# Attention B of a two-layer block: q, k and v at their own width of 64, heads worked in pairs

## The reference

```
x = x + attn_a(layernorm(x))
x = x + ffn(layernorm(x))
x = x + attn_b(layernorm(x))
x = x + ffn(layernorm(x))

attn_b(r):   # 16 heads of width 64
    q, k, v = r @ Wq + bq, r @ Wk + bk, r @ Wv + bv      # per head: 256 x 64
    pattern = softmax(causal(q @ k.T / 8))               # 256 x 256
    out = sum over heads of (pattern @ v) @ Wo  + bo     # 256 x 128
```

## Time and profile before

| | |
|---|---|
| time, median of 3 runs | 453.93 us (453.14 to 454.97) |
| the profiled execution's span | 451.1 us |
| beside its span | the time of that one execution is not listed by itself; the three timed runs lie 2.0 to 3.9 us above the span |
| PE busy | 405.4 us, 90% |
| PE weight loads busy | 359.2 us, 80% |
| ACT, DVE, POOL busy | 310.5, 307.7, 34.1 us |
| first scores, last weighted sum | 63.6 us, 424.4 us |

### The profile page before, as it was taken

How to read it: one execution, slowest core, us unless ns; L and a number is a source line. 1 busy time by engine, 2 the same in 40 slices (tenths; PEclk the granted TensorE clock), 3 DMA queues, 4 the chain that set the end, 5 groups by cost and what they waited for, 6 DMA issues and landing times.

```text
span 451.1 us, 8672 instructions
## 1 busy us (share of the span) xinstructions
PE 405.4 (90%) x2591; PEld 359.2 (80%) x2591; DVE 307.7 (68%) x1322; ACT 310.5 (69%) x945; POOL 34.1 (8%) x48
## 2 busy tenths in 40 slices
PE   0857688999999999999999999999999999999766
PEld 0756677878889988888899889888899898999545
DVE  4465538666878776977777858886786687766542
ACT  1443158797868897976768887876688888778420
POOL 4030100100000000200000002000000000000000
PEclk9998869999999999999999999999999999999955
DMA  8600000000000000000000000000000000000000
...
DMA packets 8157, 5.68 MB, mean 13 GB/s; under 512 B 944, under 2 KB 7856, under 8 KB 8112
## 3 DMA queue, kind: packets, MB, share of 16 engines
...
## 4 chain that ended last, share of the span: by engine, by line
PE 75%; ACT 10%; DVE 7%; issue 4%; DMA 2%; POOL 0%; ACTq 0%; DVEq 0%
PE bank L452 11%; PE bank L283 9%; PE bank L284 9%; PE bank L285 9%; PE bank L437 9%; PE bank L361 6%; PE bank L454 5%; PE bank L427 5%; PE bank L390 2%; DVE gated L698 2%; ACT prob L571 2%; PE bank L351 2%; DMA wv<-wv_in 2%; PE bank L306 2%; ACT gate_t L537 1%
## 5 line engine op out<-in xcount | busy, mean ns | idle before, releaser
L579 ACT ACTIVATE prob_t<-bank 128x384 f32<-128x384 f32 x128 | 62.8, 490 | 22.7 <-PE bank L437 22.5
L452 PE MATMUL bank<-prob_t,v 128*128 128x256 f32 x256 | 76.5, 381 | 0.7 <-ACT o_t L604 0.7
L437 PE MATMUL bank<-ident,prob 128*128 128x128 f32 x384 | 63.8, 275 | 4.7 <-ACT prob_t L579 4.6
L571 ACT ACTIVATE prob<-neg_s,neg_max 128x256 f32<-128x256 f32 x128 | 64.3, 503 | 0.0
L569 ACT ACTIVATE prob<-neg_s,neg_max 128x128 f32<-128x128 f32 x128 | 51.5, 403 | 12.3 <-DVE neg_max L737 12.0
L735 DVE CUSTOM_DVE_ANT_0 neg_s<-bank,mask 128x128 f32<-128x128 f32 x128 | 36.7, 287 | 33.8 <-PE bank L285 33.8
L437 PEld LDWEIGHTS bank<-ident,prob 128*128 128x128 f32 x384 | 45.4, 140 | 15.1 <-DVE prob L746 5.0
L454 PEld LDWEIGHTS bank<-prob_t,v 128*128 128x128 f32 x256 | 48.5, 190 | 6.7
L737 DVE CUSTOM_DVE_ANT_0 neg_s<-bank,mask 128x256 f32<-128x256 f32 x128 | 53.7, 420 | 0.0
L427 PE MATMUL bank<-rt,u 128*128 128x128 f32 x256 | 49.8, 276 | 0.8 <-DVE neg_max L737 0.8
L454 PE MATMUL bank<-prob_t,v 128*128 128x128 f32 x256 | 49.1, 274 | 0.0
...
## 6 DMA issues: line engine op xcount, KB each, us to landing
...
```

Of the source, the lines that this page charges most:

```text
L437: last = nc.tensor.transpose(pt_ps[:, j * P:(j + 1) * P], prob[:, k % 4, j * P:(j + 1) * P], ident[:])
L452: nc.tensor.matmul(o_ps[:, b * N:(b + 1) * N], vg[:, 2 * b, hs], prob_t[:, k % 2, 0:N], start=(step == 0), stop=False, skip_group_check=True)
L571: nc.scalar.activation(prob[:, q, P:SC], neg_s[:, r, P:SC], ACT.Exp, bias=neg_max[:, q, 1:2], scale=-1.0, accum_out=row_sum[:, q, 1:2]).th ...
L579: nc.scalar.activation(prob_t[:, k % 2, :], pt_ps[:, 0:SC], ACT.Copy).then_inc(pt_sb, 1)
```

## The change

- q, k and v are computed with the plain weights, 64 wide for a head, two heads side by side on the 128 partitions ("unit": 8 in a pair). Jobs qp and kp (X and Y) each make q^T or k^T of a unit for 512 tokens; vpX and vpY make v of 8 heads for one tile. The jobs w0 to w5 only split the weights in two halves (ACT and DVE); the products that built M and WVO are gone, and so are wb, u_low and the second copy of lntB.
- A slot is one unit and one batch: 16 slots in a pair, 64 in all, each with two heads e = 0, 1. The scores of head e contract over the 64 partitions of half e (HALVES), all in float32: rows 0 to 63 and rows 64 to 127 of PE. The weighted sum of head e has 64 output columns, which go to partitions 0 to 63 or 64 to 127 of z_ps.
- z of each unit is copied to zt by ACT (z_evac, a ring of 10), and multiplied by Wo per unit with accumulation: jobs out0 to out3, one a tile, 8 products of a tile each, and outA to outD for the last pair.
- qp, kp, vpX, vpY and the out jobs share the banks X and Y with the side jobs. Three banks now hold scores, two the transposed probabilities.
- The probabilities are scaled by POOL. Of the transposed probabilities ACT copies head 0, DVE head 1. DVE reads out kp, ACT qp, v and z.
- The transposes and the sums run LAG = 2 slots behind the scores. In a slot each engine walks its head, then the jobs of that slot (projections first, then BODY), then its tail.
- In the prologue the ACT queue issues three transfers of 512 KB (wqkv) in place of wo and two halves of wv; the SP queue issues wo, bq, bk, bv, bo in place of wk, two halves each of wq and bq, bv and bo, and no longer waits for POOL's zero fills. In EPILOGUE outB and outD stand for the two bout jobs. bo is added by POOL in lntB. The store to memory is issued in the same job as before.

```diff
 PAIRS = B * N // PAIR
 TILES = PAIR // P
 FC = F // P
-STEPS = 2 * H
-GH = PAIR // D
-GROUPS = H // GH
-CH = GROUPS * TILES
+UNITS = H // 2
+SLOTS = 2 * UNITS
+LAST = PAIRS * SLOTS
+LAG = 2
+GV = PAIR // A
+CHUNKS = H // GV * TILES
+ZR = 10
 SC = N + P
+HALVES = (slice(0, A), slice(A, P))
 EPS = 1e-5
 W_SCALE = 1.0 / 127.0
 SCORE_SCALE = A ** -0.5
...
 BODY = {
-    1: [("lns0", 1)], 3: [("lns1", 1)], 4: [("lntA", 1)], 5: [("qkv0", 1), ("qkv1", 1)], 6: [("qkv2", 1)], 7: [("mean", 1)],
-    8: [("bout", -1)], 9: [("lns0", -1)], 10: [("vwo", 1), ("lns1", -1)], 11: [("lntF", -1), ("mat0", 1)], 12: [("mat1", 1)],
-    13: [("gu0", -1)], 15: [("aout", 1), ("gu1", -1)], 17: [("lns0", 1), ("gu2", -1)], 18: [("lns1", 1)],
-    19: [("down", -1), ("lntF", 1)], 20: [("gu0", 1)], 21: [("gu1", 1)], 22: [("gu2", 1)], 23: [("down", 1)],
-    24: [("lns0", 1)], 25: [("lns1", 1)], 26: [("lntB", 1)],
+    0: [("lns0", 1), ("lns1", 1)], 1: [("lntA", 1)], 2: [("qkv0", 1), ("qkv1", 1), ("out0", -1)],
+    3: [("qkv2", 1), ("mean", 1), ("out1", -1)], 4: [("vwo", 1), ("mat0", 1), ("out2", -1)],
+    5: [("mat1", 1), ("out3", -1), ("lns0", -1)], 6: [("aout", 1), ("lns1", -1), ("lntF", -1)],
+    7: [("lns0", 1), ("gu0", -1)], 8: [("gu1", -1), ("lns1", 1)], 9: [("gu2", -1), ("lntF", 1)],
+    10: [("down", -1), ("gu0", 1)], 11: [("gu1", 1), ("gu2", 1)], 12: [("down", 1), ("lns0", 1)],
+    13: [("lns1", 1), ("lntB", 1)],
 }
-U_AHEAD, V_AHEAD = 3, 4
-T_LAG, PV_LAG = 3, 4
...
+def projections_at(m):
+
+    jobs = []
+    if 0 <= (m + 2) // 8 < 2 * PAIRS and (m + 2) % 8 < TILES:
+        jobs.append(("vpY" if m % 2 == 0 else "vpX", TILES * ((m + 2) // 8) + (m + 2) % 8, 0))
+    g, odd = divmod(m + 2, 2)
+    if g < PAIRS * UNITS:
+        jobs.append(("kp" if odd else "qp", g, 0))
+    return jobs
+
+
+def jobs_at(m):
+
+    jobs = projections_at(m)
+    p, i = divmod(m, SLOTS)
+    if m >= 0 and p < PAIRS:
+        for job, off in BODY.get(i, []):
+            if 0 <= p + off < PAIRS:
+                t0 = (p + off) * TILES
+                jobs.append((job, t0 + int(job[3]), 1) if job.startswith("out") else (job, t0, TILES))
+    if m == LAST - 1:
+        jobs += [("outA", LAST_TILE, 2), ("outC", LAST_TILE + 2, 2)]
+    return jobs
+
+
+LAST_TILE = (PAIRS - 1) * TILES
 
...
-        s_ps, pt_ps, u_ps, v_ps, o_ps, X, Y = bank[0:2], bank[2], bank[3], bank[4], bank[5], bank[6], bank[7]
...
+        s_ps, pt_ps, z_ps, X, Y = bank[0:3], bank[3:5], bank[5], bank[6], bank[7]
...
+        def s_bank(m, e):
+
+            return s_ps[(2 * m + e) % 3]
+
...
+            for m in range(-2, LAST + LAG):
+                head(m, at)
+                for job, t0, nt in jobs_at(m):
+                    side(job, t0, nt, at)
+                    at.passed(job, t0, nt)
+                tail(m, at)
...
+                elif job in ("out0", "out1", "out2", "out3", "outA", "outB", "outC", "outD"):
+                    p = t0 // TILES
+                    first = OUT_EARLY if job in ("outB", "outD") else 0
+                    end = OUT_EARLY if job in ("outA", "outC") else UNITS
+                    out, done = (Y, y_full) if job in ("outC", "outD") else (X, x_full)
+                    pe.wait_ge(z_sb, p * UNITS + end)
+                    if job == "outC":
+                        use_y(at)
+                    elif first == 0:
+                        use_x(at)
+                    for u in range(first, end):
+                        for j in tiles:
+                            last = nc.tensor.matmul(out[:, j * D:(j + 1) * D], zt[:, (p * UNITS + u) % ZR, j * P:(j + 1) * P], wo[:, u, :],
+                                                    start=(u == 0 and j == tiles[0]), stop=(u == UNITS - 1), skip_group_check=True)
+                    if end == UNITS:
...
+                elif job in ("qp", "kp"):
+                    p, u = divmod(t0, UNITS)
+                    if t0 == 0:
+                        pe.wait_ge(w_lo, 4 if job == "kp" else 2)
+                    if u == 0:
+                        rows_ready(p, at)
+                    if job == "qp":
+                        use_x(at)
+                        out, done, w = X, x_full, 0
+                    else:
+                        use_y(at)
+                        out, done, w = Y, y_full, 1
+                    us = slice(u * P, (u + 1) * P)
+                    split3(out[:], wqkv_hi[:, w, us], wqkv_lo[:, w, us], rt_hi[:, p % 2, :], rt_lo[:, p % 2, :]).then_inc(done, 1)
...
+                elif job in ("vpX", "vpY"):
+                    p, c = divmod(t0, CHUNKS)
+                    g, j = divmod(c, TILES)
+                    if t0 == 0:
+                        pe.wait_ge(w_lo, 6)
+                    if c == 0:
+                        rows_ready(p, at)
+                    if job == "vpX":
+                        use_x(at)
+                        out, done = X, x_full
+                    else:
+                        use_y(at)
+                        out, done = Y, y_full
+                    hs = slice(g * GV * A, (g + 1) * GV * A)
+                    js = slice(j * P, (j + 1) * P)
+                    split3(out[:], rt_hi[:, p % 2, js], rt_lo[:, p % 2, js], wqkv_hi[:, 2, hs], wqkv_lo[:, 2, hs]).then_inc(done, 1)
 
             def rows_ready(p, at):
...
+            def scores(m, at):
+
+                g, b = divmod(m, 2)
+                if b == 0:
+                    pe.wait_ge(x_free, at.mark["qp", g].x)
+                    pe.wait_ge(y_free, at.mark["kp", g].y)
+                if m:
+                    pe.wait_ge(s_masked, 2 * m - 1)
...
+                for e, half in enumerate(HALVES):
+                    nc.tensor.matmul(s_bank(m, e)[:, 0:P], qt[half, g % 2, t:t + P], kt[half, g % 2, t:t + P], start=True, stop=True)
+                for e, half in enumerate(HALVES):
+                    nc.tensor.matmul(s_bank(m, e)[:, P:SC], qt[half, g % 2, t + P:t + N], kt[half, g % 2, t:t + N],
+                                     start=True, stop=True).then_inc(s_full, 1)
...
+            def transposes(m):
+
+                for e in range(2):
+                    pe.wait_ge(p_norm, 2 * m + e + 1)
+                    if m:
+                        pe.wait_ge((pt_sb_a, pt_sb_b)[e], m)
+                    for j in range(3):
+                        last = nc.tensor.transpose(pt_ps[e][:, j * P:(j + 1) * P], prob[:, m % 3, e, j * P:(j + 1) * P], ident[:])
+                    last.then_inc(pt_full, 1)
...
+            def weighted_sum(m, at):
+
+                g, b = divmod(m, 2)
+                group = m // 8
+                pe.wait_ge(pt_sb_a, m + 1)
+                pe.wait_ge(pt_sb_b, m + 1)
+                if m % 8 < 2:
+                    pe.wait_ge(x_free, at.mark["vp", TILES * group + 2 * b + 1].x)
+                    pe.wait_ge(y_free, at.mark["vp", TILES * group + 2 * b + 1].y)
+                if b == 0 and g:
+                    pe.wait_ge(z_sb, g)
+                for k, cols in ((0, slice(0, N)), (1, slice(N, SC))):
+                    for e, half in enumerate(HALVES):
+                        h = (2 * g + e) % GV
+                        last = nc.tensor.matmul(z_ps[half, b * N + k * P:(b + 1) * N], v[:, group % 2, 2 * b + k, h * A:(h + 1) * A],
+                                                prob_t[:, m % 2, e, cols], start=(k == 0), stop=(k == 1), skip_group_check=True)
+                last.then_inc(pv_done, 1)
+
+            def head(m, at):
+                if 0 <= m < LAST:
+                    scores(m, at)
+                if m >= LAG:
+                    transposes(m - LAG)
+
+            def tail(m, at):
+                if m >= LAG:
+                    weighted_sum(m - LAG, at)
+
+            walk(side, head, tail)
 
 
         @block.scalar
         def _(act):
...
+            for w in range(3):
+                act.dma_start(wqkv[:, w, :], wqkv_d[:, w, :]).then_inc(ld_w, 16)
...
+                elif job == "qp":
+                    g = t0
+                    if g == 0:
+                        act.wait_ge(bq_ready, 1)
+                    act.wait_ge(x_full, at.x + 1)
+                    if g >= 2:
+                        act.wait_ge(s_full, 4 * (g - 1))
+                    u = g % UNITS
+                    nc.scalar.activation(qt[:, g % 2, :], X[:], ACT.Identity, bias=bq_s[:, u:u + 1], scale=SCORE_SCALE).then_inc(x_free, 1)
+                elif job in ("vpX", "vpY"):
+                    c = t0
+                    g, j = divmod(c, TILES)
+                    full, free, src = (x_full, x_free, X) if job == "vpX" else (y_full, y_free, Y)
+                    act.wait_ge(full, (at.x if job == "vpX" else at.y) + 1)
+                    if g >= 2:
+                        act.wait_ge(pv_done, 8 * (g - 1))
+                    nc.scalar.activation(v[:, g % 2, j, :], src[:], ACT.Copy).then_inc(free, 1)
...
+            def exp(m):
+                r, q = m % 3, m % 4
+                for e in range(2):
```

(70 more changed lines are left out.)

341 lines of the change are left out of this document (75 added, 266 removed), and 17 rows, old and new, of tables (PROLOGUE, USES).

## The result

The changed kernel takes 529.43 us (median of 4 runs, 526.91 to 534.7) against 453.6 us: a ratio of 1.168 (95% interval 1.161 to 1.175), 76 us slower. The forecast was 488, in a range of 435 to 540.

The account below looks back on a forecast made before the run. PE was taken as the bound, 90% busy at full clock. Span 451.1 + 36.6 (loop, late read-outs) - 3 (prologue) + 1 (epilogue) = 485.7 us, with 2.8 for the timed median 488; range 435 to 540.

Parts of the forecast that it names:

- The sign and the mechanism: Loop: body jobs on X and Y wait for read-outs behind ACT's exps; loop +36.6 us, slower at 0.79.
- The prices of scores, sums and transposes: PE work per slot: scores 0.9 us, weighted sums 0.8, transposes 0.66.
- POOL below 40%: Sign of being right: POOL under 40% busy and nobody waiting for it.
- half clock in a quarter of the slots: Clock rival: PE at 1.2 GHz in a quarter of the slots, +56 us, 544; chance 0.09.
- late read-out at full clock: Main case: late reads of X and Y stall PE; 488 us, own range 460 to 510, chance 0.48.
- -3 in all: Prologue: removed weight products and r copies save time, q and k reads and larger loads cost some; net -3 us.
- The slots: Inner pair counted slot by slot, from 3.8 us without PE jobs to 9.7; sum 110.7 us against 95.9.
- The trailing slots: The two slots that trail pair 3: 4 us, added to 83 for 87 against 81.2.
- POOL's scaling: Four scalings a slot, each 0 to 0.405 us, 0.8 to 1.6 in all; cost nothing.
- That PE's work decides: Rival: stalls on X and Y in slots 1 to 12 don't decide; about 400 us (399 to 450), chance 0.17.
- That halves don't overlap: Rival: scores 1.30 us and sums 1.30, 0.9 a slot more; +58, 546 us, chance 0.11.
- Gaps at every change of arrangement: Rival: three tiling-mode changes a slot at 0.16 us each, 0.5 a slot, +31; 510 to 520 us, chance 0.11.

Follow-up runs that it names:

- Two edits that undo it in different ways: On the changed kernel, exps moved behind ACT's read-outs: 492.92 us; separately, qp given its own PSUM bank, taken from the scores: 500.99 us.
- the version with extra products: Changed kernel plus 2 to 8 products without readers ahead of waiting side jobs, in prologue and loop, scores on two banks: 511.23 us, ratio 1.120.
- The fastest version: Spread side-job table, exps last, qp bank and prologue products without readers, with DVE's reciprocal moved behind the next slot's masks: 462.88 us, ratio 1.018.
- exps last: Changed kernel with exp(m) moved on ACT from the head of a slot to its tail: 492.92 us, ratio 1.084.
- a bank for qp: Changed kernel with the third score bank given to qp: 500.99 us, ratio 1.092; together with exps last 472.49 us.
- filled prologue: Exps last and qp bank together, plus products without readers in front of the prologue's jobs only: 468.17 us, ratio 1.024.
- the versions with the reciprocal and one of two other tables: On the filled-prologue version, reciprocal moved behind the next slot's masks: with the spread side-job table 462.88 us, with mean one slot later 464.01 us.

## Why the prediction was wrong

**Where it was right.** The sign and the mechanism: "the next job on X waits for qp's read-out, which stands on ACT behind both exps". Two edits that undo it in different ways gave 36.5 and 28.4 us back. The prices of scores, sums and transposes were within 0.05 us each, slots 14, 15 and 0 took 3.85 to 4.02 against 3.8 at full clock (in the version with extra products), and the epilogue 27.6 us against 27.7. POOL below 40% was wrong (43%), that nobody waits for it was right.

**The step that failed: the clock was kept out of the sum.** The prediction made it a rival of its own, "half clock in a quarter of the slots", 544 at a chance of 0.09, and gave 488 to a late read-out at full clock. But the read-out's waits make PE idle, so the two cases are not apart: of the six slots of pair 1 with a clock under 0.9, PE waits for read-outs in five, and moving the exps raised the clock in the loop from 0.93 to 0.97. (In slots 3 and 6 it waits too and stayed at 1.00, so a wait alone does not settle it.) In the prologue, where nothing of this kind was forecast, the clock was 0.50 from 24 to 69 us. With it kept at 1.00 by extra products the kernel took 18.2 us less. That is 44% of the 41 us between forecast and result; the rest is in the terms below.

**Terms that were mis-sized.** In the kernel with the extra products, at full clock, the span was 509.2 against a forecast of 485.7, and the parts compare as follows:

| part | forecast | at full clock | changed kernel |
|---|---|---|---|
| first scores | 60.6 | 66.7 | 69.4 |
| pair 0 | 89 | 91.7 | 97.0 |
| inner pairs | 110.7 each | 116.1, 116.1 | 122.7, 117.0 |
| pair 3 up to the last scores | 79 | 79.7 | 86.0 |
| from there to the end | 35.5 | 39.0 | 40.2 |

- The prologue: "-3 in all" was +5.8. The forecast took the weight products for work in the way. They had in fact filled the time between the first jobs, in which PE waits, and the clock of 0.88 and 0.99 went with them. Extra products gave 2.7 to 3.7 us back. Even so the first scores came at 66.7 and 64.9 us, 4 to 6 later than forecast; which of its terms (weight products, reads, loads) was off is open.
- The slots: 5.4 us an inner pair too few. At full clock slots 2, 3 and 4 took 9.0, 10.0 and 9.4 (counted 8.6, 9.3, 8.6), slots 9 to 11 9.1, 10.3 and 7.8 (8.4, 9.7, 6.8), the rest came within 0.25. Part of this is the extra products' own time: in pair 2 of the changed kernel slots 4, 9, 10 and 11 took 9.1, 8.6, 10.1 and 7.1, 1.8 us less in all. Undercounted were slots in which two or more reads follow each other.
- The trailing slots: from the last scores to the last weighted sum 12.7 us, in the changed kernel and at full clock alike, where 3.8 and 4 were counted. The missing term is PE's work for outA and outC, 48 instructions that stand in the last slot (timeline of the changed kernel):

```profile
493.63 5.52 PE L392 MATMUL bank<-wo,zt 128*128 128x128 f32 x48
```

  At full clock the epilogue behind it was 1.4 us shorter than forecast, so 3.5 us of the error remain.
- POOL's scaling: 0.61 and 0.93 us, not 0 to 0.405 and 0.405. This had no consequence.

**The rivals.** That PE's work decides: refuted, it would have been shown by slots of 5 us. That halves don't overlap: refuted by 0.85 against 1.38 us. Gaps at every change of arrangement (510 to 520): the rule about a drain ("TensorEngine Tiling (Array Packing)" of the Trainium skill, Key Properties) can't be told apart from the products' own ends here. Sums, scores and transposes with two of the changes took 2.28 us against a forecast of 2.36 without gaps, and the slots without side jobs, which hold all three, 3.85 to 4.02 against 3.8. So at most 0.2 us a slot was added, not 0.5. The half clock: right in kind, though it came with the read-outs and was no case beside them.

**Where the expected gain is.** PE's work of an inner pair is 84.8 us as counted. The shortest inner pairs measured took 98.8 and 96.7 us, before 95.9. The fastest version, 462.88 us, is 1.8% over the kernel before, and none beat it. Three edits took back 61 of the 76 us (exps last, a bank for qp, filled prologue); the versions with the reciprocal and one of two other tables are 4 and 5 us lower still, or 2 and 3 by the runs that the ratios take, with intervals that overlap. In the fastest version's profile, 9.1 us above that of before, the first scores come 1.2 us later, the loop takes 367.8 us against 360.8, and the epilogue 0.9 more. What the 7 us in the loop are was not separated: waits for read-outs in slots with three side jobs are still in the trace, and the granted clock there is 0.98 against 1.00.
